# Value products of two items in one group: four heads side by side in the array's four groups of 32 columns, with four buffers of probabilities

## The chip, the cores and the metric

The kernel runs on one core of one Trainium2 chip. The metric is device time in microseconds (us) of one execution; lower is better. TensorE multiplies matrices, VectorE (DVE) reduces and combines, ScalarE (ACT) applies functions, GpSimd (POOL) does small work and issues transfers, SyncE (SP) issues transfers. They run at once and meet only at semaphores.

## The reference, cut to what matters

A block of a transformer: cross attention with 16 heads of 16 channels over a short context, then a mixture of 8 experts of which each token takes two. The change touches only the attention, and in it the product of the probabilities with the values.

```python
# x: (2, 1024, 256)  context: (2, 154, 256)  16 heads of 16
qh = (layernorm(x) @ Wq.T + bq).reshape(B, 1024, 16, 16).transpose(0, 2, 1, 3)
kh = (ctx @ Wk.T + bk)...          vh = (ctx @ Wv.T + bv)...      # 154 keys
score = einsum('bhqd,bhkd->bhqk', qh, kh) / 4
attn  = softmax(where(mask, score, -10000))
out   = einsum('bhqk,bhkd->bhqd', attn, vh)                       # the value products
x = x + tanh(g_xattn) * (out @ Wo.T + bo)
x = x + tanh(g_ffn) * experts(layernorm(x))                       # top 2 of 8
```

## The kernel before, in words

The 2048 tokens are cut into 8 units of 256 (`U = 8`). A loop over frames (`for u in FRAMES`, ten of them) with ten slots each (`for i in range(ITEMS)`) sets the order on every engine by hand: each engine has its own copy of the loop, and semaphores tie them. In frame u, the scores and value products of unit u are made, the row maxima of units u+1 and u+2, and the output projection of unit u-1.

An item is what one slot's `exp` turns into probabilities, a buffer of 128 keys by 2 x 256 queries in float32. Items 1 to 4 and 6 to 9 hold two heads each over the first 128 keys ("pair"); items 0 and 5 hold the last 26 keys of eight heads ("late"). `item_heads(i)` says which.

The path of an item i: TensorE makes its scores (L1107 for a pair, L1112 for a late item) in slot i; ScalarE's `exp` (L551) writes `probs[:, g % 3]`; TensorE's value products (`softmax_v`, L1012) are made one slot later, and for item 9 at the head of the next frame, ahead of its scores. The products of a pair are two float32 matmuls with 32 columns of weights (`v_a`), each into its own 32 partitions of a bank, hence each in its own group of 32 columns of the array: `q, j = divmod(2 * n + a, 4)`, and j is the group. So items 1, 3, 6 and 8 use groups 0 and 1, items 2, 4, 7 and 9 groups 2 and 3. A late item's products use all 128 columns (`v_b`).

Between these TensorE makes the maxima's scores (`max_scores`, L1029): two a slot in slots 0 to 3 and 6 to 9, called a and b below, one ahead of the value products and one behind them. Each writes one of two banks, and waits until VectorE's `reduce_max` (L697) of the one before the last has read it. VectorE negates the 32 maxima (L705) into a tile of their own, which TensorE turns (L1056) and ScalarE rounds.

Other work in the frame that the prediction names: slot 0 turns the second layer norm's rows (L1128), slot 1 makes the gate's logits (L1136), slot 2 turns the attention output (L1034), VectorE weighs it in slot 3 (L673, L674), slot 4 turns it back (L1151), slot 5 projects it (L1159), slots 6 and 7 turn and project the queries of unit u+3 (L1042, L1050), which ScalarE and VectorE split in slot 8 (L497, L690). Weight chunks of the experts are split on the way, three or four a frame: ScalarE's half is L475, VectorE's L760. Frames with an even u do it in slots 0, 3 and 7, odd ones in 0, 3, 6 and 8, VectorE one slot later.

Of the kernel before, what the change touches and what calls it, by code (L numbers as in the profile page):

```python
# [12 lines left out]
P = 128  # L13
F32, F16, I32, U8 = mybir.dt.float32, mybir.dt.float16, mybir.dt.int32, mybir.dt.uint8
ALU = mybir.AluOpType
# [3 lines left out]
N_HEADS = 16  # L19
# [7 lines left out]
def build(nc, x, ctx, mask, g_xattn, g_ffn, wq, bq, wk, bk, wv, bv, wo, bo, wg, w1, b1, w2, b2, out):  # L27
# [7 lines left out]
    VC = 32  # L35
# [3 lines left out]
    UT = TILES_PER_UNIT * P  # L39
# [8 lines left out]
    W_CHUNK = 1024  # L48
    W_SCALE = 64.0
    PLACES = 8  # L50
    LEAD = 3
    EXPERTS_PER_LOAD = 8
    assert D == 256 and HD == 16 and 0 < S2 <= 32 and E == 8
# [14 lines left out]
    with es:  # L68
        def sb(name, shape, dt=F32):
            return es.enter_context(nc.sbuf_tensor(name, shape, dt))  # L70
# [12 lines left out]
        ident, pad_mask = sb("ident", [P, P]), sb("pad_mask", [P, 1])  # L83
# [8 lines left out]
        with ExitStack() as es_setup:  # L92
# [17 lines left out]
            v_a = [sb("v_a0", [P, N_HEADS, VC])]  # L110
            v_b = [sb("v_b0", [P, 4, 4, VC])]
# [5 lines left out]
        with ExitStack() as es_tail:  # L117
            outer, es = es, es_tail
            WT_qo = sb("WT_qo", [P, 2, KC, D])
            outT = sb("outT", [P, 2, 2 * UT])  # L120
            attn, attnT = sb("attn", [P, 2, D]), sb("attnT", [P, 2, KC, P])
            xn2 = attn
            xn2T = attnT
            stats, mv = sb("stats", [P, 2, 6]), sb("mv", [P, 2, 2])
            var, rstd, neg_half = sb("var", [P, 2]), sb("rstd", [P, 2]), sb("neg_half", [P, 2])
            recip = sb("recip", [P, 2, N_HEADS])

            with ExitStack() as es_attn:
                es = es_attn  # L130
                kst = sb("kst", [P, B, NPAIR, 2, SP], F16)
                kst_late.append(sb("kst_late1", [P, NPAIR, 2 * (SP - P)], F16))
                v_a.append(sb("v_a1", [P, N_HEADS, VC]))
                v_b.append(sb("v_b1", [P, 4, 4, VC]))
                qst = [sb(f"qst{i}", [P, NPAIR, UT], F16) for i in range(3)]
                qh, ql = sb("qh", [P, KC, UT], F16), sb("ql", [P, KC, UT], F16)
                mv1, rstd1 = sb("mv1", [P, T, 2]), sb("rstd1", [P, T])
                xn = sb("xn", [P, 2, D])
                xnT = xn
                rowmax, negmax = sb("rowmax", [P, 2 * N_HEADS]), sb("negmax", [P, 2 * N_HEADS])  # L140
                negmaxT = sb("negmaxT", [2 * N_HEADS, P], F16)
                probs = sb("probs", [P, 3, 2, UT])

            with ExitStack() as es_route:
                es = es_route
                at_place, tab_rhs = sb("at_place", [P, TOP_K * T, P], F16), sb("tab_rhs", [P, TOP_K * T, TAB], F16)
                ahead = sb("ahead", [P, T, E, E], F16)
                before, ones = sb("before", [P, P], F16), sb("ones", [P, P], F16)
                iota_slot, iota_tile = sb("iota_slot", [P, P], F16), sb("iota_tile", [P, TAB], F16)  # L150
                token_no, spare_row = sb("token_no", [P, TOP_K * T]), sb("spare_row", [P, 1])
                sig, gate_rows = sb("sig", [P, T, E]), sb("gate_rows", [P, T, E])
                rank, chosen16 = sb("rank", [P, T, E]), sb("chosen16", [P, T * E], F16)
                chosen, picked = sb("chosen", [P, TOP_K, T, E]), sb("picked", [P, TOP_K, T, E])
                n_int, n_tiles, tile_end, tile_base, no_add = (sb("n_int", [P, E], I32), sb("n_tiles", [P, E]), sb("tile_end", [P, E]),
                                                                sb("tile_base", [P, E]), sb("no_add", [P, E]))
                pos_f, local_f, place_f, base_f, tile_f = (sb(n, [P, TOP_K, T]) for n in ("pos_f", "local_f", "place_f", "base_f", "tile_f"))
                pos_i, local_i, place_i = (sb(n, [P, TOP_K, T], I32) for n in ("pos_i", "local_i", "place_i"))
                empty, token_m1 = sb("empty", [P, TAB]), sb("token_m1", [P, TAB])
                past, begun = sb("past", [P, TAB, E], F16), sb("begun", [P, TAB, E], F16)  # L160
                expert_f = sb("expert_f", [1, TAB])
            es = outer
# [10 lines left out]
        S2_BANKS, PV_BANKS, A_BANK, Q_BANK, S1_BANKS = bank[0:2], bank[2:4], bank[4], bank[5], bank[6:8]  # L173
# [17 lines left out]
        pv_evac = sem("pv_evac")  # L191
        a_filled, a_evac, q_filled, q_high, q_free = sem("a_filled"), sem("a_evac"), sem("q_filled"), sem("q_high"), sem("q_free")
        qst_landed = [sem(f"qst_landed{i}") for i in range(3)]
        max_landed = [sem(f"max_landed{i}") for i in range(3)]
        s1_filled, rowmax_done, negmax_done = sem("s1_filled"), sem("rowmax_done"), sem("negmax_done")
        s2_filled, exp_done, pv_done = sem("s2_filled"), sem("exp_done"), sem("pv_done")
# [18 lines left out]
            return X_early[:, 2 * u:2 * u + 2, :] if u < 2 else X_late[:, 2 * u - 4:2 * u - 2, :]  # L215

        ITEMS = NPAIR + 2
        FRAMES = range(U + 2)

        def live(u):  # L220
            return 0 <= u < U
# [5 lines left out]
        a_nth = {use: n + 1 for n, use in enumerate(A_USES)}  # L227
# [6 lines left out]
        def item_heads(i):  # L234

            return ("pair", i - 1 - i // 5) if i % 5 else ("late", i // 5)
# [224 lines left out]
        def _(act):  # L461
# [82 lines left out]
            for u in FRAMES:  # L544
                for i in range(ITEMS):
                    if live(u):
                        g = ITEMS * u + i
                        act.wait_ge(s2_filled, g + 1)
                        if g >= 3:
                            act.wait_ge(pv_done, g - 2)  # L550
                        nc.scalar.activation(probs[:, g % 3, :, :].rearrange("p a t -> p (a t)"), S2_BANKS[g % 2][:, :],  # L551
                                             ACT.Exp, scale=SCORE_SCALE).then_inc(exp_done, 1)
                    if u == 0 and i == 4:
                        act.wait_ge(b2_loaded, 32)
# [3 lines left out]
                    if i == 0 and live(u - 2):  # L558
                        v = u - 2
# [3 lines left out]
                    if i == 1 and live(u - 2):  # L563
                        v = u - 2
# [3 lines left out]
                    if i == 4 and live(u - 1):  # L568
                        v = u - 1
# [52 lines left out]
        def _(dve):  # L622
# [70 lines left out]

            def reduce_maxima(v, n):
                g = 2 * NPAIR * v + n
                dve.wait_ge(s1_filled, g + 1)
                nc.vector.reduce_max(rowmax[:, 2 * n:2 * n + 2],  # L697
                                     S1_BANKS[g % 2][:, 0:2 * S].rearrange("p (a s) -> p a s", a=2),
                                     AX_X).then_inc(rowmax_done, 1)

            def negate_maxima(v):
                dve.wait_ge(rowmax_done, 2 * NPAIR * (v + 1))
                if v >= 1:
                    dve.wait_ge(a_filled, a_nth["maxT", v - 1])
                nc.vector.tensor_scalar(negmax[:, :], rowmax[:, :], -1.0, None, ALU.mult).then_inc(negmax_done, 1)  # L705

            def rank_experts(tiles):

# [77 lines left out]
            for b in range(B):  # L786
                nc.vector.memset(v_b[b][:, :, :, :], 0.0)
                ins = nc.vector.memset(v_a[b][:, :, :], 0.0)
# [46 lines left out]
            for u in FRAMES:  # L835
                for i in range(ITEMS):
# [3 lines left out]
                    if i == 2 and 4 <= u + 4 < U:  # L840
                        v = u + 4
# [13 lines left out]
                    if i == 3 and live(u - 1):  # L855
                        v = u - 1
# [8 lines left out]
                    if i == 5 and live(u - 1):  # L865
                        v = u - 1
# [7 lines left out]
                    if i == 7 and live(u - 1):  # L874
                        v = u - 1
# [81 lines left out]
        def _(pe):  # L957
# [34 lines left out]
                if n >= 2:  # L992
                    pe.wait_ge(q_free, n - 1)

            def softmax_v(g):

                u, i = divmod(g, ITEMS)
                kind, n = item_heads(i)
                b = u // UNITS_PER_BATCH
                pe.wait_ge(exp_done, g + 1)  # L1000
                if i == 0 and u == 0:
                    pe.wait_ge(v_made, 2)
                if i % 5 == 0 and u >= 1:
                    pe.wait_ge(pv_evac, 2 * u - 1 + i // 5)
                for a in range(2):
                    rhs = probs[:, g % 3, a, :]
                    if kind == "pair":
                        q, j = divmod(2 * n + a, 4)
                        dst, lhs = PV_BANKS[q // 2][VC * j:VC * (j + 1), q % 2 * UT:(q % 2 + 1) * UT], v_a[b][:, 2 * n + a, :]
                    else:  # L1010
                        dst, lhs = PV_BANKS[n][:, a * UT:(a + 1) * UT], v_b[b][:, 2 * n + a, :, :].rearrange("p j c -> p (j c)")
                    ins = nc.tensor.matmul(dst, lhs, rhs, start=(i % 5 == 0 and a == 0), stop=(i % 5 == 4), skip_group_check=True)  # L1012
                ins.then_inc(pv_done, 1)

            def max_scores(v, n):

# [36 lines left out]
            def turn_maxima(v):  # L1053
                a_use("maxT", v)
                pe.wait_ge(negmax_done, v + 1)
                nc.tensor.transpose(A_BANK[0:2 * N_HEADS, 0:P], negmax[:, :], ident[:, :]).then_inc(a_filled, 1)  # L1056

            turn_x(0)
            pe.wait_ge(wT_made, 2)
# [27 lines left out]

            for u in FRAMES:
                for i in range(ITEMS):
                    if i == 0 and live(u - 1):  # L1090
                        softmax_v(ITEMS * u - 1)
                    if live(u):
                        g = ITEMS * u + i
                        b = u // UNITS_PER_BATCH
# [20 lines left out]
                    maxima = [item for item in max_items(u, i) if live(item[0])]  # L1115
                    for v, n in maxima[0:1]:
                        max_scores(v, n)
                    if i >= 1 and live(u):
                        softmax_v(ITEMS * u + i - 1)
                    for v, n in maxima[1:2]:  # L1120
                        max_scores(v, n)
                    if i == 0 and live(u - 2):
# [184 lines left out]
```

## Time and profile before

| | us |
|---|---|
| median of 3 runs | 508.83 (507.77 to 509.89) |
| the profiled execution: its own time | 510.14 |
| its span, first to last instruction | 508.3 |
| TensorE busy | 421.6 (83%) |
| VectorE busy | 314.6 (62%) |
| ScalarE busy | 218.3 (43%) |
| GpSimd busy | 181.9 (36%) |

Set-up fills the time to about 57 us, the frames run from there to about 235, the tables for the experts follow to about 260, and the experts' matmuls fill the rest. A line of the timeline reads: start, length, engine, line of the code, operation, what it writes and reads, shape, how many instructions were merged (x), and in brackets the idle time of the engine ahead of it with what ended it.
### The profile page before, as it was taken

The numbers are of one execution on the slowest core, as the hardware profiler recorded it, in microseconds if no ns is written. First come the engines' busy times: TensorE is split into PE (matmuls) and PEld (weight loads), VectorE is DVE, ScalarE is ACT, GpSimd is POOL, SyncE is SP. The second block draws the span as 40 slices with busy tenths as digits, with TensorE's granted clock in tenths as the row PEclk, the third lists the DMA queues.
The fourth block names the chain that finished last, engine by engine and source line by source line (L and its number), as shares of the span: only waits on it lengthen the run. The fifth ranks groups of instructions, "written<-read, shape, count | busy, mean of one in ns | idle before, by whom it ended". The sixth has DMA issues, their size and how long they took to land.

```text
span 508.3 us, 11089 instructions
## 1 busy us (share of the span) xinstructions
PE 421.6 (83%) x4040; PEld 323.7 (64%) x4040; DVE 314.6 (62%) x843; ACT 218.3 (43%) x549; POOL 181.9 (36%) x186
## 2 busy tenths in 40 slices
PE   5358587889898888974449999999999999999970
PEld 3234334545655445543239999999999999999960
DVE  5855668797786876468935555555555655555530
ACT  2131474565565556640016445444444444444420
POOL 8523431131231222210032554444544455544231
PEclk9855969999999999996559999999999999999995
DMA  7443232262453544412010233222333222333221
GB/s 213 99 147 113 74 130 74 89 208 95 133 171 105 145 129 129 138 72 47 1 43 24 43 52 52 50 43 44 46 53 55 43 45 43 47 51 52 25 23 19
DMA packets 35146, 40.25 MB, mean 79 GB/s; under 512 B 10432, under 2 KB 29748, under 8 KB 35092
## 3 DMA queue, kind: packets, MB, share of 16 engines
q0 software_dynamic: 12608, 27.48, 24.1%
q1 hardware_dynamic: 19953, 11.17, 7.7%
q10 hardware_dynamic: 2532, 0.89, 0.7%
q8 instruction: 34, 0.56, 0.4%
q14 instruction: 19, 0.15, 0.1%
HBM read 25.87 MB, written 9.50 MB: 70 GB/s over the span
## 4 chain that ended last, share of the span: by engine, by line
PE 67%; DVE 18%; ACT 4%; issue 4%; DMA 4%; POOL 1%; SPq 0%; ACTq 0%; DVEq 0%; POOLq 0%
PE bank L1249 7%; PE bank L1233 7%; PE bank L1234 7%; PE bank L1235 7%; PE bank L1250 6%; PE bank L1251 6%; PE bank L1012 6%; PE bank L1050 3%; PE bank L1029 3%; DVE rowmax L697 3%; PE bank L1159 3%; PE bank L1197 2%; DVE W L760 2%; PE bank L1248 2%; DMA out_rows<-y_sb,scatter_tab 2%
## 5 line engine op out<-in xcount | busy, mean ns | idle before, releaser
L1233 PE MATMUL bank<-xh,W 128*128 128x128 f16 x624 | 122.2, 221 | 1.0 <-DVE xl L927 1.0
L1234 PE MATMUL bank<-xl,W 128*128 128x128 f16 x624 | 122.2, 221 | 0.0
L1235 PE MATMUL bank<-xh,W 128*128 128x128 f16 x624 | 122.1, 221 | 0.0
L607 ACT ACTIVATE h<-bank,b1T 128x128 f32<-128x128 f32 x312 | 89.2, 369 | 70.5 <-PE bank L1235 68.5
L440 POOL DMA_INDIRECT out_rows<-y_sb,scatter_tab x39 | 63.7, 1633 | 114.1 <-DVE y_sb L944 108.0
L1249 PE MATMUL bank<-W,hh 128*128 x312 | 85.5, 274 | 0.0
L1251 PE MATMUL bank<-W,hl 128*128 x312 | 85.0, 273 | 0.0
L1250 PE MATMUL bank<-W,hh 128*128 x312 | 85.0, 273 | 0.0
L935 DVE CAST hh<-h 128x512 f16<-128x512 f32 x78 | 33.9, 434 | 76.5 <-ACT h L607 76.5
L697 DVE TENSOR_REDUCE rowmax<-bank 128x2 f32<-128x308 f32 x128 | 57.5, 473 | 25.9 <-PE bank L1029 24.7
L1233 PEld LDWEIGHTS bank<-xh,W 128*128 x624 | 61.9, 99 | 4.4 <-DVE xl L927 1.4
L1234 PEld LDWEIGHTS bank<-xl,W 128*128 x624 | 61.8, 99 | 3.5
L551 ACT ACTIVATE probs<-bank 128x512 f32<-128x512 f32 x80 | 47.3, 596 | 35.5 <-PE bank L1107 26.2
L1235 PEld LDWEIGHTS bank<-xh,W 128*128 x624 | 61.9, 99 | 0.0
L432 POOL DMA_INDIRECT xg<-xn_scratch,gather_tab x39 | 44.8, 1148 | 41.4 <-DVE gather_tab L915 22.9
L937 DVE TENSOR_TENSOR hl<-h,hh 128x512 f16<-128x512 f32 x78 | 54.0, 693 | 2.7
L359 POOL DMA_DIRECT2D W_stage<-in_L_ffn_W x32 | 21.6, 675 | 92.7 <-DVE W L760 91.5
L1029 PE MATMUL bank<-kst,qst 97*128 97x308 f16 x128 | 40.2, 324 | 11.9 <-DVE rowmax L697 11.5
L1012 PE MATMUL bank<-probs,v_a 128*32 128x256 f32 x256 | 42.1, 410 | 7.1 <-ACT probs L551 7.0
L589 ACT ACTIVATE xh<-bank 128x256 f16<-128x256 f32 x39 | 15.0, 384 | 75.0 <-PE bank L1197 74.9
L760 DVE SCALAR_TENSOR_TENSOR W<-W_stage,W 128x1024 f16<-128x1024 f32 x28 | 35.1, 1255 | 7.1 <-ACT W L475 7.0
L1029 PEld LDWEIGHTS bank<-kst,qst 97*128 97x128 f16 x128 | 12.2, 98 | 39.2 <-DVE rowmax L697 29.1
(187 smaller groups left out, 667.1 us busy)
## 6 DMA issues: line engine op xcount, KB each, us to landing
W_stage<-in_L_ffn_W POOLq DMA_DIRECT2D x32, 512.0 KB, 4.1
xn_scratch<-attn SPq DMA_DIRECT2D x8, 256.0 KB, 2.2
qst<-qh SPq DMA_DIRECT2D x60, 32.0 KB, 2.5
X_late<-in_x SPq DMA_DIRECT2D x6, 256.0 KB, 5.8
out_rows<-X_late SPq DMA_DIRECT2D x6, 256.0 KB, 2.5
qst<-ql SPq DMA_DIRECT2D x28, 32.0 KB, 2.9
xg<-xn_scratch,gather_tab POOLq DMA_INDIRECT x39, 3.0
out_rows<-y_sb,scatter_tab POOLq DMA_INDIRECT x39, 3.9
```

The lines of the kernel that those rows point to most:

```text
L440: nc.gpsimd.indirect_dma_start(out=out, out_offset=bass.IndirectOffsetOnAxis(ap=scatter_tab[:, t:t + 1], axis=0), in_=y_sb[t % 3][:, :], i ...
L607: ins = nc.scalar.activation(h32[s % 4][:, m * P:(m + 1) * P], H_BANKS[s % 4][:, m * P:(m + 1) * P], ACT.Gelu_apprx_tanh, scale=1.0 / W_SC ...
L697: nc.vector.reduce_max(rowmax[:, 2 * n:2 * n + 2], S1_BANKS[g % 2][:, 0:2 * S].rearrange("p (a s) -> p a s", a=2), AX_X).then_inc(rowmax_d ...
L937: nc.vector.tensor_tensor(hl[s % 4][:, :], h32[s % 4][:, :], hh[s % 4][:, :], ALU.subtract).then_inc(hl_made, 1)
L1012: ins = nc.tensor.matmul(dst, lhs, rhs, start=(i % 5 == 0 and a == 0), stop=(i % 5 == 4), skip_group_check=True)
L1029: nc.tensor.matmul(S1_BANKS[g % 2][:, 0:2 * S].rearrange("p (a s) -> p a s", a=2), qst[v % 3][0:ROW_MAX, p, j * P:(j + 1) * P], kst[0:ROW_ ...
L1233: nc.tensor.matmul(dst, wh, xh[t % 3][:, cut], start=(c == 0), stop=False)
L1234: nc.tensor.matmul(dst, wh, xl[t % 3][:, cut], start=False, stop=False)
L1235: ins = nc.tensor.matmul(dst, wl, xh[t % 3][:, cut], start=False, stop=(c == KC - 1))
L1249: nc.tensor.matmul(y, hh[s % 4][:, cut], both[0], start=False, stop=False)
L1250: nc.tensor.matmul(y, hh[s % 4][:, cut], both[1], start=False, stop=False)
L1251: ins = nc.tensor.matmul(y, hl[s % 4][:, cut], both[0], start=False, stop=(m == FC - 1))
```

## The change

The value products of two items are made in one slot, right behind each other: items 1 and 2 in slot 3, 3 and 4 in slot 5, 6 and 7 in slot 8, 8 and 9 in slot 0 of the next frame, now behind that frame's first scores and its maximum a. The late items stay where they were (slots 1 and 6). The four heads of such a group write four different groups of 32 columns. Since an item's probabilities may now wait a slot longer, there are four buffers for them instead of three. The negated maxima are written over the maxima, so their tile goes, and the wait for the earlier transpose moves from the negation to the next unit's first `reduce_max`.

```diff
+    PROBS = 4
...
-                probs = sb("probs", [P, 3, 2, UT])
+                probs = sb("probs", [P, PROBS, 2, UT])
...
+        VALUE_SLOTS = {0: (8, 9), 1: (0,), 3: (1, 2), 5: (3, 4), 6: (5,), 8: (6, 7)}
...
-                        if g >= 3:
-                            act.wait_ge(pv_done, g - 2)
-                        nc.scalar.activation(probs[:, g % 3, :, :].rearrange("p a t -> p (a t)"), S2_BANKS[g % 2][:, :],
+                        if g >= PROBS:
+                            act.wait_ge(pv_done, g - PROBS + 1)
+                        nc.scalar.activation(probs[:, g % PROBS, :, :].rearrange("p a t -> p (a t)"), S2_BANKS[g % 2][:, :],
...
+                if n == 0 and v >= 1:
+                    dve.wait_ge(a_filled, a_nth["maxT", v - 1])
...
-                if v >= 1:
-                    dve.wait_ge(a_filled, a_nth["maxT", v - 1])
-                nc.vector.tensor_scalar(negmax[:, :], rowmax[:, :], -1.0, None, ALU.mult).then_inc(negmax_done, 1)
+                nc.vector.tensor_scalar(rowmax[:, :], rowmax[:, :], -1.0, None, ALU.mult).then_inc(negmax_done, 1)
...
-            def softmax_v(g):
+            def softmax_v(u, items):
...
-                pe.wait_ge(exp_done, g + 1)
+                pe.wait_ge(exp_done, ITEMS * u + items[-1] + 1)
...
+                for i in items:
+                    kind, n = item_heads(i)
+                    for a in range(2):
+                        rhs = probs[:, (ITEMS * u + i) % PROBS, a, :]
...
+                ins.then_inc(pv_done, len(items))
...
-                    if i == 0 and live(u - 1):
-                        softmax_v(ITEMS * u - 1)
...
-                    if i >= 1 and live(u):
-                        softmax_v(ITEMS * u + i - 1)
+                    w = u if i else u - 1
+                    if i in VALUE_SLOTS and live(w):
+                        softmax_v(w, VALUE_SLOTS[i])
```

How this moves TensorE's instructions, at two places. The first is slots 1 to 5 of a full frame on TensorE; a row is line, operation, what it writes from what, and its size. Before:

```order
L1012 MATMUL bank<-probs,v_b 128x256 x2
L1029 MATMUL bank<-kst,qst 128x308
L1136 MATMUL bank<-wg_sb,attnT 128x8 x4
L1107 MATMUL bank<-qst,kst 128x256 x2
L1029 MATMUL bank<-kst,qst 128x308
L1012 MATMUL bank<-probs,v_a 32x256 x2
L1029 MATMUL bank<-kst,qst 128x308
L1034 MATMUL bank<-ident,outT 128x128 x8
L1107 MATMUL bank<-qst,kst 128x256 x2
L1029 MATMUL bank<-kst,qst 128x308
L1012 MATMUL bank<-probs,v_a 32x256 x2
```

The same place in the changed kernel, where lines stand one or two higher:

```order
L1014 MATMUL bank<-probs,v_b 128x256 x2
L1031 MATMUL bank<-kst,qst 128x308
L1137 MATMUL bank<-wg_sb,attnT 128x8 x4
L1107 MATMUL bank<-qst,kst 128x256 x2
L1031 MATMUL bank<-kst,qst 128x308 x2
L1036 MATMUL bank<-ident,outT 128x128 x8
L1107 MATMUL bank<-qst,kst 128x256 x2
L1031 MATMUL bank<-kst,qst 128x308
L1014 MATMUL bank<-probs,v_a 32x256 x4
```

Slot 2 has lost its value products, and slot 3 has four heads where it had two. In the same way slot 4 loses its two heads and slot 5 has four.

The second place is TensorE from slot 8 to slot 0 of the next frame. Before:

```order
L1107 MATMUL bank<-qst,kst 128x256 x2
L1029 MATMUL bank<-kst,qst 128x308
L1012 MATMUL bank<-probs,v_a 32x256 x2
L1029 MATMUL bank<-kst,qst 128x308
L1107 MATMUL bank<-qst,kst 128x256 x2
L1029 MATMUL bank<-kst,qst 128x308
L1012 MATMUL bank<-probs,v_a 32x256 x2
L1029 MATMUL bank<-kst,qst 128x308
L1012 MATMUL bank<-probs,v_a 32x256 x2
L1112 MATMUL bank<-qst,kst_late 64x256 x4
L1029 MATMUL bank<-kst,qst 128x308 x2
L1128 MATMUL bank<-ident,attn 128x128 x4
```

In the changed kernel:

```order
L1107 MATMUL bank<-qst,kst 128x256 x2
L1031 MATMUL bank<-kst,qst 128x308
L1014 MATMUL bank<-probs,v_a 32x256 x4
L1031 MATMUL bank<-kst,qst 128x308
L1107 MATMUL bank<-qst,kst 128x256 x2
L1031 MATMUL bank<-kst,qst 128x308 x2
L1112 MATMUL bank<-qst,kst_late 64x256 x4
L1031 MATMUL bank<-kst,qst 128x308
L1014 MATMUL bank<-probs,v_a 32x256 x4
L1031 MATMUL bank<-kst,qst 128x308
L1129 MATMUL bank<-ident,attn 128x128 x4
```

Slot 9 has no value products now, and those of items 8 and 9 stand between the two maxima of slot 0, where before those of item 9 stood ahead of both and of the scores.

## Rows read from the trace of the kernel before

**Rows 1.** Busy time by stretch: span, then each engine, clock, DMA share, GB/s.

```profile
105.00:125.00 20.00, 18.49 (x127) 11.59 (x125) 15.52 (x38) 11.99 (x22) 4.85 (x8) 1.00 0.47 146
```

**Rows 2.** Timeline, TensorE: one pair of heads and one late item.

```profile
180.81 1.03 PE L1012 MATMUL bank<-probs,v_b 128*128 128x256 f32 x4
181.67 0.30 PE L1029 MATMUL bank<-kst,qst 97*128 97x308 f16 x1
...
182.79 0.30 PE L1029 MATMUL bank<-kst,qst 97*128 97x308 f16 x1 [0.60 <-DVE rowmax L697]
183.02 0.41 PE L1012 MATMUL bank<-probs,v_a 128*32 128x256 f32 x2
183.26 0.39 PE L1012 MATMUL bank<-probs,v_a 128*32 128x256 f32 x2
183.58 0.30 PE L1029 MATMUL bank<-kst,qst 97*128 97x308 f16 x1
183.72 0.38 PE L1107 MATMUL bank<-qst,kst 113*128 113x256 f16 x2
```

**Rows 3.** Chain that ended last, slots 1 to 3 of frame 4: start, length, what.

```profile
150.92 0.56 PE bank L1012 x4
...
151.71 0.88 PE bank L1034 x8
...
152.94 0.56 PE bank L1012 x4
...
153.77 0.49 DVE rowmax L697
```

**Rows 4.** Timeline, slot 4 of frame 4: what ends TensorE's wait.

```profile
155.86 0.63 PE L1151 MATMUL bank<-ident,attn 128*128 128x128 f32 x4 [1.34 <-DVE attn L674]
```

**Rows 5.** Timeline, slot 7 of frame 4, TensorE and VectorE.

```profile
161.08 1.32 DVE L697 TENSOR_REDUCE rowmax<-bank 128x2 f32<-128x308 f32 x3
...
161.59 0.30 PE L1029 MATMUL bank<-kst,qst 97*128 97x308 f16 x1 [0.16 <-DVE rowmax L697]
...
162.38 0.30 PE L1029 MATMUL bank<-kst,qst 97*128 97x308 f16 x1
```

**Rows 6.** Timeline, from slot 9 of frame 4 into frame 5.

```profile
166.63 0.63 PE L1012 MATMUL bank<-probs,v_a 128*32 128x256 f32 x4
...
168.48 0.69 PE L1029 MATMUL bank<-kst,qst 97*128 97x308 f16 x2 [0.89 <-DVE rowmax L697]
169.01 0.60 PE L1128 MATMUL bank<-ident,attn 128*128 128x128 f32 x4
```

**Rows 7.** Timeline, from slot 9 of frame 3 into frame 4.

```profile
146.63 0.63 PE L1012 MATMUL bank<-probs,v_a 128*32 128x256 f32 x4 [0.78 <-ACT probs L551]
...
147.88 1.40 DVE L697 TENSOR_REDUCE rowmax<-bank 128x2 f32<-128x308 f32 x3
...
148.47 0.30 PE L1029 MATMUL bank<-kst,qst 97*128 97x308 f16 x1
```

**Rows 8.** Timeline, frame 0, slots 5 to 7.

```profile
71.43 0.58 ACT L551 ACTIVATE probs<-bank 128x512 f32<-128x512 f32 x1
...
72.46 1.56 PE L1012 MATMUL bank<-probs,v_b 128*128 128x256 f32 x4
...
74.98 0.48 DVE L697 TENSOR_REDUCE rowmax<-bank 128x2 f32<-128x308 f32 x1 [0.32 <-PE bank L1029]
```

**Rows 9.** Timeline, frames 5, 6 and 7: waits beside value products.

```profile
187.76 0.48 DVE L697 TENSOR_REDUCE rowmax<-bank 128x2 f32<-128x308 f32 x1 [0.31 <-PE bank L1029]
...
204.24 1.11 PE L1012 MATMUL bank<-probs,v_a 128*32 128x256 f32 x8 [0.36 <-ACT probs L551]
...
212.95 0.63 PE L1012 MATMUL bank<-probs,v_a 128*32 128x256 f32 x4
```

**Rows 10.** Timeline, TensorE's wait in frame 1.

```profile
86.15 0.30 PE L1029 MATMUL bank<-kst,qst 97*128 97x308 f16 x1 [2.17 <-DVE rowmax L697]
```

**Rows 11.** Busy time by stretch behind that wait, columns as in 1.

```profile
87.18:90.60 3.42, 3.42 (x17) 2.04 (x16) 2.71 (x8) 1.25 (x2) 1.51 (x3) 0.50 0.44 116
```

More of the change, by code:

```diff
@@ L139, in build @@
                 xnT = xn
-                rowmax, negmax = sb("rowmax", [P, 2 * N_HEADS]), sb("negmax", [P, 2 * N_HEADS])
+                rowmax = sb("rowmax", [P, 2 * N_HEADS])
                 negmaxT = sb("negmaxT", [2 * N_HEADS, P], F16)
-                probs = sb("probs", [P, 3, 2, UT])
+                probs = sb("probs", [P, PROBS, 2, UT])
             with ExitStack() as es_route:
@@ L993, in q_use @@
                     pe.wait_ge(q_free, n - 1)
-            def softmax_v(g):
-                u, i = divmod(g, ITEMS)
-                kind, n = item_heads(i)
+            def softmax_v(u, items):
                 b = u // UNITS_PER_BATCH
-                pe.wait_ge(exp_done, g + 1)
-                if i == 0 and u == 0:
+                pe.wait_ge(exp_done, ITEMS * u + items[-1] + 1)
+                if items[0] == 0 and u == 0:
                     pe.wait_ge(v_made, 2)
[L1003 to L1013, printed above, removed]
+                if items[0] % 5 == 0 and u >= 1:
+                    pe.wait_ge(pv_evac, 2 * u - 1 + items[0] // 5)
+                for i in items:
+                    kind, n = item_heads(i)
+                    for a in range(2):
+                        rhs = probs[:, (ITEMS * u + i) % PROBS, a, :]
+                        if kind == "pair":
+                            q, j = divmod(2 * n + a, 4)
+                            dst, lhs = PV_BANKS[q // 2][VC * j:VC * (j + 1), q % 2 * UT:(q % 2 + 1) * UT], v_a[b][:, 2 * n + a, :]
+                        else:
+                            dst, lhs = PV_BANKS[n][:, a * UT:(a + 1) * UT], v_b[b][:, 2 * n + a, :, :].rearrange("p j c -> p (j c)")
+                        ins = nc.tensor.matmul(dst, lhs, rhs, start=(i % 5 == 0 and a == 0), stop=(i % 5 == 4), skip_group_check=True)
+                ins.then_inc(pv_done, len(items))
             def max_scores(v, n):
@@ L1055, in turn_maxima @@
                 pe.wait_ge(negmax_done, v + 1)
-                nc.tensor.transpose(A_BANK[0:2 * N_HEADS, 0:P], negmax[:, :], ident[:, :]).then_inc(a_filled, 1)
+                nc.tensor.transpose(A_BANK[0:2 * N_HEADS, 0:P], rowmax[:, :], ident[:, :]).then_inc(a_filled, 1)
             turn_x(0)
```

## The prediction

> **What bounds the kernel now.** The change touches the frames alone, 57 to 235 us, so I read the stretches first: between 105 and 125 us TensorE is busy 18.49 of 20 us and VectorE 15.52, at the full clock, 2.4 GHz [rows 1]. TensorE is nearest to being the bound, with VectorE close. A share doesn't say where a saved microsecond comes through, so next comes the chain that ended last: in slots 1 to 3 of a frame it stays on TensorE, and the two value products there are on it with 0.56 us each [rows 3]; then VectorE takes over with the last maximum of slot 3. Last come the timelines around every place where value products leave: does TensorE or VectorE hold the next step there?
>
> **What one group of value products costs.** Maximum to maximum around a pair of heads is 183.58 - 182.79 = 0.79 us [rows 2], and the second maximum takes 183.72 - 183.58 = 0.14 by itself, so the pair costs 0.65. Inside, both heads' first passes start at 183.02 and both second passes at 183.26: two heads stream at once, in 0.24 a pass. The late item with all 128 columns takes (181.67 - 180.81) / 4 = 0.215 a pass with nothing beside it. So the two heads' passes are 0.48 of the 0.65, and 0.17 goes into and out of the narrow weights. If four heads stream as two do, a group of four costs 0.65 as well, and each merging saves 0.65. There are 4 a unit and 8 units: 32 x 0.65 = 20.8 us of TensorE's time. Most of it isn't on the path.
>
> No row shows four heads at once. The bounds: nothing more (two heads already differ from one by only 0.025 a pass, a fixed amount rather than a share), or 0.48 more (two of the four groups stream at a time). I take 0.03, near the low end, since the two heads there show no sharing of a stream and four more weight loads have to be started.
>
> The Trainium skill ("TensorE: Matmul & The Clock Gate", Part 3, the table of measured speedups) gives 2.38 times for three column tiles. By that an estimate is 3 / 2.38 = 1.26 times one matmul's time, some 0.54 for the two passes instead of 0.48; the sum below would lose another half microsecond. The trace has two tiles only and can't confirm it.
>
> **The change place by place**, each as gain in us on the path. Frames and slots are those of the code.
> - *Slot 2, frames 1 to 6.* The pair between L1029 and L1034 goes. TensorE holds the chain there, and VectorE has the maxima of slot 1 done by then; with 0.65 less VectorE's idle time before the maxima of slot 3 only shrinks. The probabilities of item 2 are ready well before slot 3. Gain 6 x 0.65 = 3.9.
> - *Slot 4.* Its pair moves into slot 5. Here TensorE waits for VectorE's weighing of the output anyway (1.34 idle ahead of L1151 [rows 4]), so nothing is gained, and the wait grows to 1.34 + 0.56 = 1.90. In slot 5 a group stands where a pair stood: no loss but the 0.03.
> - *Slot 7, frames 1 to 4.* The pair goes, but maximum b needs VectorE's read of the second of three: 161.08 + 2/3 x 1.32 = 161.96, so b can go at 162.00 instead of 162.38 [rows 5]. Gain 4 x 0.38 = 1.5, passed on through L1050, the query's split and VectorE behind it.
> - *Slots 8 and 9.* Four heads stand in slot 8, ahead of maximum b, as two did; slot 9 loses its pair. VectorE, with the split of the query and a weight chunk, is what TensorE waits for next: no gain.
> - *Turn into odd frames 1, 3, 5.* Before, item 9's products ran at 166.63, inside TensorE's wait for VectorE; maximum a waited until 168.48 and L1128 came at 169.01 [rows 6]. Now the group stands behind that maximum: 168.48 + 0.14 + 0.65 + 0.14 = 169.41. Loss 3 x 0.40 = 1.2: work that was covered comes into the open.
> - *Turn into even frames 2, 4.* The products waited 0.78 for the exp before the scores; the scores and maximum a now fill that wait. But the next maximum, at 148.47, needs VectorE's read from 147.88 (its first of three ends at 148.35) [rows 7]. Gain 0.
> - *Frame 0.* The pair of slot 4 goes; the late products of slot 6 at 72.46 can follow the exp's end at 72.01, 0.45 earlier; then slot 7 gives the full 0.65, since VectorE idles there (0.32 [rows 8]). Gain 1.1.
> - *Frame 5, slots 7 and 9.* No query is made, and VectorE loses the idle time of 0.31 behind each removed pair, of which one is shown [rows 9]. Gain 0.6.
> - *Frame 6 end, frame 7.* The 0.36 wait for the exp ahead of item 9's products [rows 9] is filled by the next scores: 0.35. In frame 7 there are no maxima; slot 2's pair (0.65) and a wait beside it go, and items 3 and 4 come behind the exp of item 4 as item 4 did at 212.95: 0.8. Its slots 6 to 9 hang on ScalarE: 0.
> - *The dearer group:* slot 3 in 7 frames, slot 5 in 8, slot 0 in 3: 18 x 0.03 = 0.5 lost.
> - *Fourth buffer, maxima in place.* Exp of item g now waits for products of g-4. The tightest, item 7 for item 3, is made in slot 5, two slots earlier, as before. The moved VectorE wait asks for L1056 of slot 5, which TensorE has issued before the very maximum that VectorE reduces in slot 6. Both cost 0; if one bound, VectorE's three maxima and everything behind them in slot 7 [rows 5] would be late by it.
>
> Sum: 3.9 + 1.5 - 1.2 + 1.1 + 0.6 + 0.35 + 0.8 - 0.5 = 6.55, say 6.6 us. The profiled execution's own time is 510.14, 1.3 above the median of 508.83; the sum is a difference inside its span of 508.3, and I take it from the median: 508.8 - 6.6 = **502.2 us**. The experts' part doesn't change.
>
> **The rivals.**
> *Four don't stream at once.* If two groups stream at a time, each group of four costs 0.48 more. At the 18 places on the path that is 8.6 us against 7.05 won: 510.4, and up to 512.5 with slot 8's maximum b (0.1 a frame) and slots 3 and 0 passing it on to VectorE. For it: no row shows more than two. Against: two cost almost what one does. It decides from 7.05 / 18 = 0.39 a group. This is the one that ends slower. Chance 0.11.
>
> *The clock falls.* After TensorE idled 2.17 us in frame 1 [rows 10], the granted clock was 0.50, that is 1.2 GHz, from 87.18 to 90.60 [rows 11]. After idling 1.34 in slot 4 [rows 4] it stayed at full speed: 20 us with such a wait show 1.00 [rows 1]. The change makes that wait 1.90, between the two, in six frames. A fallen stretch of 3.4 us at half speed, where L1151 to L1159 hold the path, costs 3.4 / 2 = 1.7. In one to three of the frames: 504 to 507.3; in all six 512. Chance 0.15. The Trainium skill (the same page, Part 4) says that transposes don't count as work for the clock in the same way; L1151, right behind the wait, is one, and by that rule the fall would be likelier, with three frames at 507.3. No row here separates transposes from other work. The other way, a little less cold time around 63 to 73 and 87 to 91 us could give 1.7 more.
>
> *It doesn't do what it says for the end.* VectorE paces the frames more than the chain shows and the gaps return as waits on its maxima: 507 to 509. The chain in slots 1 to 3 is against it. Chance 0.07.
>
> *TensorE is the bound throughout*, and all 20.8 come through: 488. The waits there are against it [rows 4 to 7]. Chance 0.01.
>
> My forecast has 0.66, with a range of its own from 499.5 to 504.5: every place without its doubtful half (slot 7, frames 0, 5, 6 and 7 halved: 2.2 less), or with the turn's loss gone and a cold stretch less. Over all cases, leaving out the slow ends of the first two rivals, the range is 498.5 to 507.5. A measurement of this kernel tells about 0.5%, 2.5 us, from no change. Faster by more than that: 0.66, nearly all of the clock's 0.15 and a part of the third, 0.79; within: 0.13; slower: 0.08.
>
> **What would show it.** In the profile of the changed kernel: four heads' first passes within some 0.03 us of each other, and maximum to maximum around them 0.8 to 0.85; half as much busy time of the narrow value products. Frames shorter by about 0.65 + 0.38 where they turn into even ones and 0.6 where into odd ones. TensorE's wait ahead of L1151 (L1152 there) at 1.9. L1128's successor in odd frames 0.4 later after maximum a. A clock of 0.50 anywhere between 95 and 220 us would be the second rival; starts of the passes in twos, 0.48 apart, the first. What makes it wrong: either of these, or waits on maxima in slot 3.

## The result, and the profile after

The changed kernel is slower: 519.6 us median (517.6 to 521.9, 4 runs) against 509.4 (507.8 to 510.9, 4 runs), a ratio of 1.0206 with a 95% interval of 1.0177 to 1.0235. The forecast was 502.2, with a range up to 507.5. The profiled execution took 517.62, its span is 515.9. Here and below, ratios leave out the slow executions, those more than 1.5% above the fastest of the same kernel (four of ten in fill_both, the profiled one among them, two of ten in group_ahead), while medians are of all.

First the forecast's cheap part, the group of four heads itself. The timeline of TensorE in slot 3 of frame 2 (all eight records of the group merged), and a narrow cut of another group, in slot 8 of frame 3:

```profile
110.92 0.29 PE L1031 MATMUL bank<-kst,qst 97*128 97x308 f16 x1
111.15 0.64 PE L1014 MATMUL bank<-probs,v_a 128*32 128x256 f32 x8
111.72 0.30 PE L1031 MATMUL bank<-kst,qst 97*128 97x308 f16 x1
111.86 0.38 PE L1107 MATMUL bank<-qst,kst 113*128 113x256 f16 x2
...
148.37 0.42 PE L1014 MATMUL bank<-probs,v_a 128*32 128x256 f32 x4
```

Maximum to maximum is 0.80 us, less 0.14 for the maximum is 0.66: four heads cost what two did (0.65 [rows 2]). The last line says why: the records of four first passes lie within 0.42 us, and one pass by itself is 0.40 to 0.41 long. The four column groups stream at once, and a group cost 0.01 more than a pair, where I had charged 0.03.

Now busy time by stretch (columns as in [rows 1]): 20 us as there, one frame at full speed (from its turned maxima in slot 5 to the next frame's), and three stretches behind waits.

```profile
105.00:125.00 20.00, 17.00 (x117) 11.31 (x118) 14.83 (x37) 11.65 (x22) 4.84 (x8) 0.91 0.46 138
...
114.60:118.02 3.42, 3.42 (x19) 1.72 (x18) 1.44 (x2) 1.17 (x2) 0.60 (x1) 0.50 0.08 13
128.26:131.67 3.41, 3.41 (x18) 2.12 (x19) 1.32 (x4) 1.38 (x3) 1.66 (x2) 0.50 0.67 210
138.50:141.91 3.41, 3.41 (x19) 1.71 (x19) 1.50 (x3) 1.17 (x2) 0.81 (x1) 0.50 0.07 8
...
143.20:163.68 20.48, 17.14 (x126) 11.14 (x125) 16.54 (x36) 13.10 (x23) 5.29 (x7) 1.00 0.47 134
```

The granted clock is 0.50, 1.2 GHz, in stretches that the kernel before didn't have: it was at 1.00 from 90.6 to 227 us. The frame without such a stretch takes 20.48 us, against 20.84 for the same one before; that with two of them (from 119.23 to 143.20) takes 23.97 against 21.21. What TensorE did ahead of each fall stands in the timeline: the wait in slot 4, and the turn into frame 3.

```profile
114.41 0.92 PE L1152 MATMUL bank<-ident,attn 128*128 128x128 f32 x4 [2.17 <-DVE attn L676]
115.26 0.64 PE L1112 MATMUL bank<-qst,kst_late 113*64 113x256 f16 x4
115.83 1.08 PE L1014 MATMUL bank<-probs,v_a 128*32 128x256 f32 x8
116.84 2.56 PE L1160 MATMUL bank<-WT_qo,attnT 128*128 128x256 f32 x8
...
126.09 0.41 PE L1112 MATMUL bank<-qst,kst_late 113*64 113x256 f16 x4
128.19 0.41 PE L1031 MATMUL bank<-kst,qst 97*128 97x308 f16 x1 [1.69 <-DVE rowmax L701]
128.54 1.08 PE L1014 MATMUL bank<-probs,v_a 128*32 128x256 f32 x8
...
160.39 0.63 PE L1152 MATMUL bank<-ident,attn 128*128 128x128 f32 x4 [1.90 <-DVE attn L676]
...
161.85 1.99 PE L1160 MATMUL bank<-WT_qo,attnT 128*128 128x256 f32 x8
```

The wait ahead of L1152 is 1.90 in frame 4, as forecast to the hundredth, and 2.17 in frames 2 and 3, where 1.90 was forecast too; the wait at the turn has grown from 0.89 [rows 6] to 1.69. Behind the wait that ends at 114.41 all is slow: the group takes 1.08 where a group at full speed takes 0.64, the projection L1160 2.56 instead of 1.99 (frame 4, last line). These are the instructions that hold the path there.

### The profile page after: what moved, and what is told of

Read it like the earlier page. It is cut to its first block, busy times and chain, and to the rows that moved or that the text cites. A ratio compares the mean times of both kernels' runs of the same rounds, so it can differ in the third digit from the quotient of the medians.

```text
span 515.9 us, 11088 instructions
## 1 busy us (share of the span) xinstructions
PE 421.2 (82%) x4040; PEld 328.7 (64%) x4040; DVE 313.5 (61%) x843; ACT 218.8 (42%) x549; POOL 182.1 (35%) x186
## 4 chain that ended last, share of the span: by engine, by line
PE 63%; DVE 21%; DMA 5%; issue 4%; ACT 3%; POOL 1%; SPq 0%; ACTq 0%; DVEq 0%; POOLq 0%
PE bank L1250 7%; PE bank L1234 7%; PE bank L1236 7%; PE bank L1235 7%; PE bank L1252 6%; PE bank L1251 6%; PE bank L1014 4%; DVE rowmax L701 4%; PE bank L1160 4%; PE bank L1052 3%; DVE W L762 3%; DMA W_stage<-in_L_ffn_W 3%; PE bank L1031 3%; DVE stats L641 2%; PE bank L1198 2%
## 5 line engine op out<-in xcount | busy, mean ns | idle before, releaser
L609 ACT ACTIVATE h<-bank,b1T 128x128 f32<-128x128 f32 x312 | 88.9, 369 | 70.3 <-PE bank L1236 68.4
L1031 PE MATMUL bank<-kst,qst 97*128 97x308 f16 x128 | 42.1, 345 | 18.0 <-DVE rowmax L701 17.0
L477 ACT ACTIVATE W<-W_stage 128x1024 f16<-128x1024 f32 x32 | 33.7, 1054 | 6.6 <-DMA W_stage<-in_L_ffn_W 6.6
```

The source lines that it names most:

```text
L609: ins = nc.scalar.activation(h32[s % 4][:, m * P:(m + 1) * P], H_BANKS[s % 4][:, m * P:(m + 1) * P], ACT.Gelu_apprx_tanh, scale=1.0 / W_SC ...
L1031: nc.tensor.matmul(S1_BANKS[g % 2][:, 0:2 * S].rearrange("p (a s) -> p a s", a=2), qst[v % 3][0:ROW_MAX, p, j * P:(j + 1) * P], kst[0:ROW_ ...
```

## The experiments

Two theories were to be told apart. A: the order is as good as forecast, and the loss is the clock, which falls behind TensorE's waits (at first I put that down to their length, from merge_12_only on to how little TensorE does around them). B: groups of four, standing elsewhere, hold up VectorE or ScalarE.

To compare traces without the start-up (the turned maxima of frame 0 stand anywhere from 68.4 to 73.1 us in them), I measure from the turned maxima of frame 1 to those of frame 6 (L1056 or L1058 in slot 5): five full frames. Their rows, columns as in [rows 1], for the kernel before, the changed one, then fill_slot4, fill_both, pair_back_slot4 and group_ahead:

```profile
96.24:200.54 104.30, 91.31 (x614) 56.08 (x613) 80.81 (x180) 61.83 (x110) 25.93 (x37) 1.00 0.46 137
```
```profile
97.63:210.35 112.72, 93.89 (x615) 60.22 (x613) 80.02 (x180) 62.92 (x110) 25.92 (x37) 0.88 0.42 126
```
```profile
97.94:200.31 102.37, 88.70 (x664) 59.85 (x663) 79.97 (x180) 62.95 (x110) 25.97 (x37) 0.98 0.47 139
```
```profile
95.98:198.72 102.74, 91.34 (x684) 61.81 (x683) 80.07 (x180) 62.77 (x110) 25.96 (x37) 0.98 0.49 139
```
```profile
94.46:198.03 103.57, 87.49 (x614) 56.81 (x613) 79.98 (x180) 62.82 (x110) 25.92 (x37) 0.97 0.45 133
```
```profile
92.82:199.62 106.80, 90.98 (x614) 58.51 (x613) 80.06 (x180) 62.59 (x110) 25.92 (x37) 0.94 0.45 134
```

The first number behind the stretch is its length, the one behind POOL's count the mean granted clock. The five frames grew from 104.3 to 112.7 us, 8.4 of the 10.2 in the medians. A mean clock of 0.88 is 27 us at half speed, eight stretches of 3.4. That the profiled execution isn't an odd one is shown by the mean clock of each whole execution: 0.863 to 0.872 in the four of the changed kernel, 0.895 to 0.917 in those of the kernel before, 0.880 to 0.899 in those of fill_slot4.

**fill_slot4.** The changed kernel with extra matmuls behind the scores of slot 4, inside the wait:

```diff
                         ins.then_inc(s2_filled, 1)
+                        if i == 4 and u >= 1:
+                            pe.wait_ge(exp_done, g)
+                            for _ in range(10):
+                                nc.tensor.matmul(S2_BANKS[(g + 1) % 2][:, 0:UT], kst[0:ROWS, b, 0, 0, 0:P], qst[u % 3][0:ROWS, 0, :],
+                                                 start=True, stop=True)
```

> The changed kernel with ten extra matmuls (256 columns, half precision, 0.107 us each, into a bank of scores that is free then and is overwritten) behind the scores of slot 4, inside TensorE's wait for VectorE; nothing else moves. Theory A, the clock: the changed kernel loses its time because TensorE's waits of 1.90 to 2.17 us in slot 4 let the granted clock fall to half behind them. Then the falls behind slot 4 go (four or five of the eight between 90 and 210 us), each worth up to 1.7 us: about 519.6 - 8 = 511 to 513. Theory B, the order: groups of four and their place hold up VectorE or ScalarE. Then the extra work changes nothing or costs: 519 to 522.

Measured: 509.6 us median, ratio to the kernel before 1.0007 (0.9967 to 1.0046). The five frames take 102.4 us, 10.3 less than without the extra work, and hold one stretch at half speed instead of eight. Doing more made it faster. The median is below A's 511 to 513, since the falls at the turns of frames went too, though nothing was added there: in this execution the waits of 1.69 and 1.70 us that end at 127.0 and 168.6 stayed without a fall.

**fill_both.** Ten more at the turn, `if i == 0 and u % 2 == 1 and u < 7`.

> As the run before, and ten more of these matmuls in slot 0 of frames 1, 3 and 5, behind the first scores, where TensorE waits 1.69 us for VectorE. Theory A: nearly no stretch at half clock is left between 95 and 225 us, and the time is near the forecast of 502, with 0.4 us more for each of the three frames if the extra work reaches past the wait: 502 to 506. Theory B: 519 or more.

Measured: 508.1, ratio 0.9924 (0.9888 to 0.996); the median of the kernel before was 509.9 in this round, so by medians the gain is 0.4%. The five frames take 102.7 us, and one stretch at half speed is left in them, as in fill_slot4. Theory B, by which neither should have gained anything, has fallen with these two. But 508 isn't 502 to 506: the order itself gives less than forecast. That is taken up below.

**pair_back_slot4.** `VALUE_SLOTS = {0: (8, 9), 1: (0,), 3: (1, 2), 4: (3,), 5: (4,), 6: (5,), 8: (6, 7)}`.

> The changed kernel with item 3's products back in slot 4 and item 4's alone in slot 5; the other three groups of four stay. TensorE's wait in slot 4 becomes 1.34 us again. Theory A: as the first fill, without any extra work, about 511 to 513. Theory B: one merging of four undone gives back a quarter of the loss of 10: about 517.

Measured: 512.7, ratio 1.0057 (1.0024 to 1.0089); five frames in 103.6 us, two stretches at half speed, one behind the turn at 123.5. Within A's 511 to 513.

**group_ahead.** As that, and the group of items 8 and 9 ahead of maximum a:

```diff
+                    if i == 0 and live(u - 1):
+                        softmax_v(u - 1, (8, 9))
                     for v, n in maxima[0:1]:
                         max_scores(v, n)
```

> As the run before, and the group of items 8 and 9 in slot 0 stands ahead of maximum a instead of behind it, so that it is done inside TensorE's wait at the turn of frames. Two groups of four stay in the open (slots 3 and 8), two are where pairs were. Theory A: no new fall of the clock, no loss at the turn: 500 to 503, faster than before by 6 to 8. Theory B: about 514, since two of four mergings still stand in changed places.

Measured: 507.9, ratio 0.9937 (0.989 to 0.9984), runs from 501.4 to 511.1. Slightly better than the kernel before, but neither A's 500 to 503 nor B's 514, and A's "no new fall" was wrong: the profiled execution has four.

```profile
109.81 0.63 PE L1154 MATMUL bank<-ident,attn 128*128 128x128 f32 x4 [1.74 <-DVE attn L676]
110.37 0.64 PE L1112 MATMUL bank<-qst,kst_late 113*64 113x256 f16 x4
...
123.61 0.83 PE L1031 MATMUL bank<-kst,qst 97*128 97x308 f16 x2 [1.13 <-DVE rowmax L701]
```
```profile
110.30:113.71 3.41, 3.41 (x14) 1.88 (x13) 1.14 (x2) 1.17 (x2) 0.60 (x1) 0.50 0.16 48
123.96:127.37 3.41, 3.38 (x12) 2.75 (x13) 1.42 (x3) 2.03 (x3) 1.37 (x2) 0.50 0.68 206
```

One lies behind a wait of 1.74, another behind one of 1.13 at the turn, while in the kernel before six waits of 1.34 to 1.35 and one of 1.37 passed without a fall. So the length of the wait alone isn't what decides.

**merge_34_only.** The kernel before, but with four buffers and the maxima negated in place, and the one merging in slot 5: `{1: (0,), 2: (1,), 3: (2,), 5: (3, 4), 6: (5,), 7: (6,), 8: (7,), 9: (8,)}`, item 9 at the head of slot 0.

> The kernel before (with four buffers and the maxima negated in place) and one merging alone: item 3's products leave slot 4 and stand with item 4's in slot 5. By my sum this costs nothing in itself; TensorE's wait in slot 4 grows from 1.34 to 1.90 us. Theory A, the clock: falls of the granted clock to half appear behind slot 4 in four or five frames, up to 1.7 us each: 514 to 518. Theory B, the order of the turn of frames and of slots 3 and 8 is what costs: the time is that of the kernel before, 509 to 511.

Measured: 514.8, ratio 1.0105 (1.0035 to 1.0174), in A's range. The profiled execution, the fastest of its runs at 510.95, shows the wait of 1.90 in all six frames, but a fall behind only two of them (at 91.4, ahead of the five frames, and at 135.8), where A expected four or five. One of those without a fall:

```profile
112.82 0.63 PE L1154 MATMUL bank<-ident,attn 128*128 128x128 f32 x4 [1.90 <-DVE attn L676]
```

and the mean clock over the five frames is 0.98:

```profile
95.26:201.60 106.34, 90.40 (x615) 56.45 (x614) 80.80 (x180) 61.73 (x110) 25.97 (x37) 0.98 0.45 129
```

**merge_12_only.** On the same ground, one merging, in slot 3: `{1: (0,), 3: (1, 2), 4: (3,), 5: (4,), 6: (5,), 7: (6,), 8: (7,), 9: (8,)}`, item 9 at the head.

> The kernel before (with four buffers and the maxima negated in place) and one merging alone: items 1 and 2 in slot 3. By my sum it wins 0.65 us in each of frames 1 to 6, 3.9 in all, and TensorE's wait in slot 4 stays near 1.34. Refined theory A (what counts is how little TensorE does around a wait, not the wait alone): the pair missing in slot 2 brings some falls behind slot 4 even at the short wait; one to three of them, so 507 to 511. If the wait's length alone counted, no fall and about 507. Where VectorE takes the moments of a later unit in slot 2 (frames 1 to 3) it should be the bound, TensorE's wait in slot 4 should be 1.6 and the gain 0.27 less.

Measured: 506.9, ratio 0.996 (0.9928 to 0.9993). One new fall, at 133.9, behind a slot 4 wait of 1.62. The frames: from frame 4's to frame 5's turned maxima 20.55 us instead of 21.20, which is the 0.65; from 1 to 2 20.47 instead of 20.85, 0.38 = 0.65 - 0.27; the wait in slot 4 is 1.62 in frames 2 and 3, 1.35 in 4 to 6. The 0.27 holds. From 3 to 4 it is only 20.78 instead of 20.84; there VectorE waited 0.61 for ScalarE's half of a weight chunk. Between the refined theory and the wait's length this run doesn't decide: the median is at the edge of both forecasts, and the one fall lies behind a wait of 1.62, longer than the 1.34 or 1.35 that passed without one.

**two_column_groups.** The changed kernel with `q, j = n // 4 * 2 + n % 2, n // 2 % 2 * 2 + a`: the four heads of a group use two column groups. The heads' outputs are permuted, so what follows the attention computes with other numbers.

> The changed kernel with the heads of a group of four in two groups of 32 columns instead of four (the heads' outputs land in other places of the same banks, so the attention output is of permuted heads). It shows what four side by side are worth. If four stream at once in the changed kernel, a group takes 0.65 + 0.48 = 1.13 us here. At 18 places on the path that is 8.6 more; but TensorE idles less, so fewer falls of the clock may give part of it back: 521 to 528. If the column groups don't matter: 519.6.

Measured: 522.7, ratio 1.028 (1.019 to 1.037). The same place as above, slot 3 of frame 2:

```profile
111.78 0.29 PE L1031 MATMUL bank<-kst,qst 97*128 97x308 f16 x1
112.01 1.06 PE L1014 MATMUL bank<-probs,v_a 128*32 128x256 f32 x8
113.00 0.30 PE L1031 MATMUL bank<-kst,qst 97*128 97x308 f16 x1
113.14 0.38 PE L1107 MATMUL bank<-qst,kst 113*128 113x256 f16 x2
```

and its five frames:

```profile
98.02:211.09 113.07, 95.67 (x615) 61.10 (x613) 79.97 (x180) 63.63 (x110) 25.95 (x37) 0.94 0.43 126
```

(1.22 - 0.14) = 1.08 us a group against 0.66. The five frames take 0.35 us more than the changed kernel's, not ten times 0.42 more: TensorE is busier (95.7 us against 93.9), and four stretches at half speed are left instead of eight, a mean clock of 0.94 instead of 0.88.

**before_filled.** The kernel before with eight of the extra matmuls in slot 4.

> The kernel before with eight extra matmuls (256 columns, half precision) in TensorE's wait of 1.34 us in slot 4. Theory A: there is no fall to be avoided there, so the time stays at that of the kernel before, 508 to 511. If instead extra work in the wait brings time in some other way than by the clock, this kernel is faster by several us as well.

Measured: 510.7, ratio 0.9988 (0.9951 to 1.0026); five frames in 104.9 us, against 104.3. Extra work gained nothing here, where there was no fall to prevent.

**ahead_and_filled.** group_ahead with fills: ten in slot 4, eight in slot 0 of frames 1, 3, 5, six in slots 7 and 9 of frames 6 and 7.

> The kernel that puts the group of items 8 and 9 ahead of the maxima and item 3 back into slot 4, with extra matmuls in TensorE's waits: ten in slot 4, eight in slot 0 of frames 1, 3 and 5, six in slots 7 and 9 of frames 6 and 7. Theory A: its four falls of the clock between 105 and 200 us go, each worth up to 1.7 us: 501 to 504. Theory C, the weight chunks' transfers bind now that frames are shorter (ScalarE waited 4 us in all for them in that kernel, 0.4 in the kernel before): the falls go but the time stays above 505.

Measured: 506.5, ratio 0.9918 (0.9882 to 0.9955).

```profile
95.10:195.89 100.79, 92.95 (x681) 61.93 (x679) 79.78 (x180) 62.82 (x110) 25.92 (x37) 0.98 0.49 140
```

The five frames take 100.8 us, 3.5 less than in the kernel before, with one stretch at half speed. The falls went but the time stayed above 505, as C had it, and outside A's 501 to 504. What the trace shows of C is small, though: ScalarE's longest wait for a weight chunk is 0.83 us, so how much of the miss is C's stays open.

**moments_later.** That kernel with VectorE's moments at `if i == 4` instead of `if i == 2`.

> The kernel ahead_and_filled with VectorE's moments of the later unit (frames 0 to 3) taken in slot 4 instead of slot 2. In the changed kernel TensorE's wait in slot 4 was 2.17 us in frames 2 and 3 and 1.90 in frames 4 to 6, and the difference of 0.27 is where my forecast of those frames fell short. If the moments in slot 2 are the cause, frames 1 to 3 get shorter by 0.27 each, 0.8 in all. Rival: the shortfall is from the transfers of weight chunks; then nothing changes, or GpSimd, which waits for the moments ahead of its next chunk, makes it longer.

Measured: 504.8, ratio 0.99 (0.9874 to 0.9926). From frame 1 to 2 19.80 us instead of 20.06, from 2 to 3 20.18 instead of 20.43: 0.26 and 0.25, as expected. From 3 to 4 it is 20.55 instead of 20.15: there VectorE waited 0.78 for ScalarE's half of a weight chunk at 147.52, where it had waited 0.39, so the rival, too, had a part. The five frames end 0.1 shorter, not the 0.8 that was expected, and don't account for a median 1.7 below that of ahead_and_filled.

**warm_before_experts.** ahead_and_filled with extra matmuls beside those of the experts' tables and during the first gather, and with TensorE's waits for the weights ahead of the tables.

> The kernel ahead_and_filled with extra matmuls where TensorE waits for the experts' tables: two of 128 columns beside each small matmul of the table, and 28 of 256 columns while the first rows are gathered. Theory A, that TensorE's own work holds the clock up: the experts' stretch begins at 2.4 GHz instead of 7 us later, which is worth half of that, 2 to 3.5 us: 503 to 504.5. If the extra matmuls run past the gathering they cost up to 2 us instead.

Measured: 503.3, ratio 0.9858 (0.9807 to 0.9909), 4 runs from 501.1 to 505.1. In the profiled execution the extra matmuls bring the clock to 1.00 from 246.6 to 256.8 us, a stretch that ahead_and_filled spends at 0.50; but then it falls again and stays at 0.50 until 263.6, while that of ahead_and_filled has it back at 261.5 (in the kernel before it was 268.1):

```profile
256.80:263.60 6.80, 5.79 (x54) 5.72 (x54) 1.48 (x7) 3.21 (x8) 2.17 (x3) 0.50 0.21 60
```

and this execution took 505.06, no less than ahead_and_filled's profiled one with 504.71. The two faster executions (501.1 and 501.6) have a mean clock of 0.928 and 0.929, the two slower ones (504.9 and 505.1) of 0.917 and 0.915: the time again goes with the clock. Whether this addition brings anything stays open; it is the fastest kernel of the study by its median, but its runs and those of ahead_and_filled overlap.

## Why the prediction was wrong

**What failed** is first the price of the clock. The sum put it at nothing and left it to a rival: "In one to three of the frames: 504 to 507.3; in all six 512. Chance 0.15." It came, and larger: eight stretches at half speed in five frames, 10.3 us. Second, the path's sum was too large as well: with the clock kept up, the order gives 1.9 us over five frames where its terms make 4.3, and the filled kernels' 509.6 and 508.1 lie outside the range too. That part is taken apart under "Point by point". In the clock's rival three things were off.

- *It judged by the length of one wait.* I set 1.90 between 1.34 (no fall) and 2.17 (fall) and asked which side it lies on. The runs show that the wait alone doesn't decide: six waits of 1.90 with two falls in merge_34_only, falls behind 1.74 and 1.13 in group_ahead, none behind 1.69 in fill_slot4. In slot 9 of frame 5 the kernel before waited longer, without a fall, than the changed one with:

```profile
186.63 0.30 PE L1029 MATMUL bank<-kst,qst 97*128 97x308 f16 x1 [1.37 <-DVE rowmax L697]
```
```profile
193.23 0.82 PE L1031 MATMUL bank<-kst,qst 97*128 97x308 f16 x2 [1.22 <-DVE rowmax L701]
```

What changed everywhere is that TensorE has less to do around its waits: between 105 and 125 us it was busy 18.49 of 20 us before, 17.00 after, the slow stretch included. That this is what lowers the clock fits the runs that added work: the fills (one stretch instead of eight) and two_column_groups (four). It isn't shown in itself: no run changes the moment of a wait and leaves the work around it as it is.
- *It looked at slot 4 only.* The item "turn into odd frames" counted 0.40 us for covered work coming into the open. It missed that this work, with the late scores, had broken up TensorE's wait there, which grew from 0.89 to 1.69. Of the eight new stretches at half speed four lie behind slot 4 (114.6, 138.5, 182.9, 206.8), two at such turns (128.3, 172.6), and a double one runs from slot 9 of frame 5 over the turn into frame 6 (193.1 to 199.9).
- *Its number.* The size, 3.4 / 2 = 1.7 us a stretch, was near: the changed kernel's five frames lose 10.3 us by eight stretches against fill_slot4's one, 10.3 / 7 = 1.5. But there were eight, not one to three, nor one in each of six frames.

**Point by point.** Slot 2: 0.65 a frame, right from frame 4 to 5 (merge_12_only, 21.20 to 20.55), and 0.38 in frames where VectorE also takes moments (1 to 3). I wrote that VectorE's idle time ahead of slot 3's maxima only shrinks; in these frames there was not enough of it. First the kernel before, frame 2, then the changed one, where VectorE has no idle time left:

```profile
111.72 0.48 DVE L697 TENSOR_REDUCE rowmax<-bank 128x2 f32<-128x308 f32 x1 [0.24 <-PE bank L1029]
```
```profile
110.26 0.86 DVE L701 TENSOR_REDUCE rowmax<-bank 128x2 f32<-128x308 f32 x2
111.03 0.74 DVE L641 BATCH_NORM_STATS2 stats<-X_late 128x6 f32<-128x256 f32 x2
111.81 0.25 DVE L644 BATCH_NORM_AGGREGATE mv<-stats 128x2 f32<-128x6 f32 x2
111.97 0.83 DVE L701 TENSOR_REDUCE rowmax<-bank 128x2 f32<-128x308 f32 x2
```

That is 3 x 0.27 = 0.8 of the 3.9, and it is also the 2.17 where 1.90 was forecast. Moving the moments away gave 0.26 a frame back.

Slot 4 and 5 (no gain, wait of 1.90): right. The turn into odd frames: from frame 4 to 5, fill_slot4 takes 20.61 and ahead_and_filled, whose group stands ahead of the maximum, 20.17: 0.44 for the forecast's 0.40. Slot 7: not isolated by a run; from frame 4 to 5 ahead_and_filled wins 21.20 - 20.17 = 1.03, which is 0.65 + 0.38. Group price: 0.66 against 0.68. The frames 0, 5, 6 and 7: not tested one by one. Waits for weight chunks, which I had left out of the sum: ScalarE waited once for 1.19 us in the changed kernel,

```profile
154.40 1.06 ACT L477 ACTIVATE W<-W_stage 128x1024 f16<-128x1024 f32 x1 [1.19 <-DMA W_stage<-in_L_ffn_W]
```

and in fill_both twice about 1 us. They reach the path: VectorE then waits for ScalarE's half,

```profile
155.49 1.23 DVE L762 SCALAR_TENSOR_TENSOR W<-W_stage,W 128x1024 f16<-128x1024 f32 x1 [0.71 <-ACT W L477]
```

and from frame 3 to 4, where the terms 0.65 and 0.38 would make 20.84 - 1.03 = 19.81 us, the frame is longer by about that wait in these traces: 20.48 in the changed kernel (wait 0.71), 20.70 in fill_slot4 (0.91), 20.24 in fill_both (0.46), 20.15 in ahead_and_filled (0.39), 20.55 in moments_later (0.78).

Over the five frames the forecast's own terms make 5 x 0.65 + 4 x 0.38 + 0.6 - 2 x 0.40 - 0.3 = 4.3 us; with the clock kept up, fill_slot4 has 1.9 and fill_both 1.6. In fill_slot4 the moments take 0.5, the chunk from frame 3 to 4 takes 0.9, and the one stretch at half speed that is left, from frame 5 to 6, about 0.9 (20.10 us there, 19.19 in group_ahead without one): 4.3 - 2.3 = 2.0. In fill_both the sum is the same with 0.4 for that chunk and 0.7 for a second one at 108.25, 1.8. So the terms come out within 0.2 us over these frames, and what the sum lacked are the moments and the chunks. Outside the five frames it isn't separated: from frame 0 to 1, where 1.1 was to be won, fill_slot4 takes 25.52 us against 24.65, with the clock at 0.50 for 9.2 us of it against 5.4. The rival to which my text gave the slower end, two groups streaming at a time, was not the cause: two_column_groups is what it would have been, and it is another 3 us slower.

What stays open is what exactly makes the clock fall behind one wait and not behind another. Executions of one kernel differ by up to 10 us here (501.4 to 511.1 for group_ahead), and the profile shows one of them.

## What to carry to other kernels

Taking work off TensorE can cost more than it gives when the work isn't on the path: in this kernel, where TensorE waits often, its own work kept its clock up. Before shortening it, list its idle times and add up what is left around each, and if the clock falls, put matmuls nobody needs into the waits, as fill_slot4 did for 10 us. When work is merged, ask of each place it leaves whether it was covered, and of each place it goes to whether it will be: the same group cost 0.4 us behind the maximum and nothing ahead of it.

## What the hardware showed that I hadn't expected

- Four float32 matmuls of 32 columns, each in its own column group, take 0.66 us for a group of four heads where two heads take 0.65, and four in only two groups 1.08. The estimate from the Trainium skill's 2.38 times for three column tiles ("TensorE: Matmul & The Clock Gate", Part 3), which the prediction gave beside its own, isn't borne out by this: only 0.01 was lost with four.
- The granted clock came down to 1.2 GHz behind waits of 1.13 to 1.74 us in one order of instructions (group_ahead) and stayed at 2.4 GHz behind six of 1.34 to 1.35 and one of 1.37 in the kernel before and four of 1.90 in merge_34_only. In "Why this matters for your kernels" the Trainium skill ("TensorE: Matmul & The Clock Gate") warns of idle gaps between bursts of matmuls that are longer than any of these. Here falls came behind shorter ones, so the measurement decides.
- Ten matmuls of 256 columns in slot 4's wait shortened five frames by 10.3 us; eight of them in the kernel before, where the clock didn't fall, changed nothing that can be told from noise (ratio 0.9988, 0.9951 to 1.0026).
